# Three half-size products in place of four in the lower left quarter of a Toeplitz convolution, with the low half of the operand made by an adding transfer

## What is computed

```python
kv = jnp.einsum('bhil,bhjl->bijhl', k_, v_)          # here k = v = ctx: symmetric in i, j
y = irfft(rfft(kv, n=2 * L) * rfft(ssm_kernel, n=2 * L))[..., :L]   # causal convolution along l
out = y + kv * D[None, None, None, :, None]
out = jnp.einsum('bijhl,bhil->bjhl', out, q_)         # q = layernorm(x)
x = x + jnp.tanh(g_xattn[0]) * out
```

## Time and profile before

| | |
|---|---|
| median of 3 runs | 4437.81 us (4437.43 to 4440.19) |
| the profiled execution's own time | 4438.08 us |
| span of its trace | 4436.3 us |
| mean granted TensorE clock | 0.991 |
| TensorE busy | 4317.6 us, 97% of the span |
| VectorE busy | 2749.1 us, 62% (nearly all the time up to 2120 us, about a quarter behind) |
| ScalarE busy | 1477.2 us, 33% |
| GpSimd busy | 879.4 us, 20% |
| the 16 transfer engines | some 38% of the span |

### The profile page before, as it was taken

The page is one execution under the profiler, slowest core; times in us unless marked ns, Lnnn a source line. Parts: engine busy times, 40 slices in busy tenths (PEclk is TensorE's granted clock), DMA queues, the critical chain, the costliest instruction groups (busy, mean ns, idle before and its releaser), DMA issues.

```text
span 4436.3 us, 72403 instructions
## 1 busy us (share of the span) xinstructions
PE 4317.6 (97%) x27466; PEld 3963.1 (89%) x27466; DVE 2749.1 (62%) x2977; ACT 1477.2 (33%) x2003; POOL 879.4 (20%) x1072
## 2 busy tenths in 40 slices
PE   7999999999999999999599999999999999999997
PEld 7999999999999999999478887888898988988986
DVE  7999999999999999999443442222233233233232
ACT  4555554555545555454211111111121121121120
POOL 1222222222122222222000004443001111111111
PEclk9999999999999999999799999999999999999999
DMA  3333333333334333333713233344244344344332
GB/s 108 114 118 106 115 111 113 118 109 114 109 113 118 109 115 109 112 118 90 138 58 114 77 95 100 98 106 111 74 140 99 76 114 99 76 114 99 76 95 48
DMA packets 227122, 457.67 MB, mean 103 GB/s; under 512 B 41744, under 2 KB 107770, under 8 KB 226998
## 3 DMA queue, kind: packets, MB, share of 16 engines
q1 hardware_dynamic: 200150, 388.45, 30.4%
q0 software_dynamic: 26848, 67.41, 7.5%
HBM read 285.86 MB, written 169.89 MB: 103 GB/s over the span
## 4 chain that ended last, share of the span: by engine, by line
PE 47%; DMA 2%; DVE 1%; issue 1%; ACT 0%; SPq 0%; POOL 0%; DVEq 0%; POOLq 0%; ACTq 0%
PE moe_ps L1497 11%; PE moe_ps L1498 11%; PE moe_ps L1499 11%; PE moe_ps L1515 4%; PE moe_ps L1517 4%; PE moe_ps L1516 4%; PE moe_psT L1486 1%; DMA out<-moe_y,moe_add_i 1%; DMA out<-moe_y 1%; DVE moe_zl L1395 1%; DMA moe_y<-out 0%; ACT moe_zh L1167 0%; DVE moe_hid L1408 0%; DVE moe_y L1422 0%; DMA moe_zin<-zT_d 0%
## 5 line engine op out<-in xcount | busy, mean ns | idle before, releaser
L592 PE MATMUL att_psY<-att_kv_hi,att_tz_hi 128*128 128x288 f32 x4608 | 1395.5, 303 | 31.5 <-DVE att_kv_lo L463 31.5
L593 PE MATMUL att_psY<-att_kv_lo,att_tz_hi 128*128 128x288 f32 x4608 | 1359.7, 295 | 0.0
L594 PE MATMUL att_psY<-att_kv_hi,att_tz_lo 128*128 128x288 f32 x4608 | 1355.9, 294 | 0.0
L592 PEld LDWEIGHTS att_psY<-att_kv_hi,att_tz_hi 128*128 128x128 f32 x4608 | 865.3, 188 | 43.7 <-issue 43.7
L1497 PE MATMUL moe_ps<-moe_zh,moe_w1h 128*128 128x512 f32 (+2 forms) x2368 | 860.6, 363 | 33.6 <-DVE moe_zl L1395 21.8
L594 PEld LDWEIGHTS att_psY<-att_kv_hi,att_tz_lo 128*128 128x128 f32 x4608 | 868.0, 188 | 0.0
L593 PEld LDWEIGHTS att_psY<-att_kv_lo,att_tz_hi 128*128 128x128 f32 x4608 | 867.6, 188 | 0.0
L1498 PE MATMUL moe_ps<-moe_zl,moe_w1h 128*128 128x512 f32 (+2 forms) x2368 | 858.8, 363 | 0.0
L1499 PE MATMUL moe_ps<-moe_zh,moe_w1l 128*128 128x512 f32 (+2 forms) x2368 | 856.4, 362 | 0.0
L1408 DVE TENSOR_TENSOR moe_hid<-moe_ps,moe_act_s 128x512 f32<-128x512 f32 (+2 forms) x148 | 91.6, 619 | 882.3 <-PE moe_ps L1499 857.9
L352 ACT ACTIVATE att_y<-att_psY 128x576 f32<-128x576 f32 x512 | 332.1, 649 | 703.7 <-PE att_psY L594 702.9
(11 more groups left out here) (168 smaller groups left out, 5213.8 us busy)
## 6 DMA issues: line engine op xcount, KB each, us to landing
att_kT<-in_cT SPq DMA_DIRECT2D x64, 512.0 KB, 4.2
att_xn<-in_x SPq DMA_DIRECT2D x64, 512.0 KB, 5.8
att_tz_hi<-filt_hi SPq DMA_DIRECT2D x64, 512.0 KB, 3.7
att_tz_lo<-filt_lo SPq DMA_DIRECT2D x64, 512.0 KB, 4.8
out<-att_x SPq DMA_DIRECT2D x64, 512.0 KB, 4.0
z_d<-att_z SPq DMA_DIRECT2D x64, 512.0 KB, 3.7
zT_d<-att_zT SPq DMA_DIRECT2D x64, 512.0 KB, 4.9
moe_zin<-zT_d SPq DMA_DIRECT2D x64, 512.0 KB
```

Source lines behind the costliest of these rows:

```text
L592: nc.tensor.matmul(acc, tz_hi[u][:, d:d + P], hi, start=(c == 0), stop=False)
L593: nc.tensor.matmul(acc, tz_hi[u][:, d:d + P], lo, start=False, stop=False)
L594: last = nc.tensor.matmul(acc, tz_lo[u][:, d:d + P], hi, start=False, stop=(c == a))
```

## The change

The lower left quarter of the matrix (sums a = 4 to 7, key tiles c = 0 to 3) has 16 block products, built from T1 to T7. The change computes it with three products of half the size. With d(0) = k(0) - k(2) and d(1) = k(1) - k(3) it forms V0 = T4 d(0) + T3 d(1) and V1 = T5 d(0) + T4 d(1) (function `shared`). Sum 4 is V0 plus S-blocks on k(2), k(3) plus its own T-blocks, sum 6 is minus V0 plus S-blocks on k(0), k(1) plus its own; sums 5 and 7 do the same with V1. The S-blocks are S(d) = T(d) + T(d-2), made once for all heads in `prepare_filters`. That is 12 block products for the quarter, and 32 for the head.

What comes with it: `differences` and `low_u` on VectorE (L568, L576; 1152 elements a partition), `high_u` on ScalarE (L418), and `minus_v` on ScalarE (L435, four copies of 288 columns a head), which writes the negative of V from `psY[0]` to `psY[1]` in PSUM. The far sums are built on top of it, in the order 0, 1, 2, 3, 4, 6, 5, 7. The Toeplitz arrays shrink to 768 columns each, and `load_sums` fetches two arrays of 640 columns into one buffer.

The low part of half 1 of `kv` is no longer subtracted by VectorE. ScalarE writes -kv_hi into `kv_lo` (`minus_high`, L410), and GpSimd issues a transfer of 1152 KB that adds `kv` to it in SBUF (`add_low`, L355). The fifth sum, `pairs(.., 1)` and `squares(.., 1)` wait for its landing (`lo_in`).

The hand-written orders change as well. VectorE begins a step with `pairs(h+1, 0)` and the statistics of x; `low(h+1)` and `low_u(h+1)` stand at its end. ScalarE begins with the squares, and rounds half 0 between the first two sums. On TensorE `turn_o(h-1, 0)` and `turn_z(h-2, 1)` move behind the second sum of the next head, and `turn_o(h-1, 1)` between the two halves of the sixth.

```diff
...
+TAPS = 896
+SUMS = 768
+PAD = TAPS + SUMS
...
+    TW = 6 * P
+    SW = 5 * P
+    def toeplitz(filt, first, width):
+        return bass.AP(filt.tensor, first, [[PAD, H], [1, P], [1, width]])
+    t_hi, t_lo = toeplitz(filt_hi, 0, TW), toeplitz(filt_lo, 0, TW)
+    s_hi, s_lo = toeplitz(filt_hi, TAPS, SW), toeplitz(filt_lo, TAPS, SW)
+    ORDER = (0, 1, 2, 3, 4, 6, 5, 7)
+    def blocks(a):
+        if a < G:
+            return [("T", a - c, c) for c in range(a + 1)]
+        far = [("S", a + 2 - c, c) for c in (2, 3)] if a < 6 else [("S", a - c, c) for c in (0, 1)]
+        return far + [("T", a - c, c) for c in range(G, a + 1)]
...
+            def load_sums(h):
+                wait(sp, y_done, NT * h)
+                sp.dma_start(sz_hi[:, :].bitcast(F32), s_hi[h]).then_inc(sz_in, 16)
+                sp.dma_start(sz_lo[:, :].bitcast(F32), s_lo[h]).then_inc(sz_in, 16)
...
+            def add_low(h, u):
+                pool.wait_ge(minus_set, h + 1)
+                pool.sem_inc(passed, 1)
+                nc.gpsimd.dma_start(
+                    kv_lo[u][:, keys_of(1)].rearrange("p t b i -> p (t b i)").rearrange("p (x n) -> p x n", x=2).bitcast(F32),
+                    kv[1][:, :, :, :].rearrange("p t b i -> p (t b i)").rearrange("p (x n) -> p x n", x=2),
+                    accum_op=ALU.add, max_dma_last_dim=8192).then_inc(lo_in, 16)
+            add_low(0, 0)
             def step(h, u, ahead, back, back2):
+                roots(0, h)
                 if back:
                     roots(1, h - 1)
                 if ahead:
-                    roots(0, h + 1)
+                    add_low(h + 1, 1 - u)
...
+            def minus_high(h, u):
+                act.wait_ge(hi_set, 2 * h + 2)
+                nc.scalar.activation(kv_lo[u][:, keys_of(1)].rearrange("p t b i -> p (t b i)"),
+                                     kv_hi[u][:, keys_of(1)].rearrange("p t b i -> p (t b i)").bitcast(F32),
+                                     ACT.Copy, scale=-1.0).then_inc(minus_set, 1)
...
+            def conv_out(h, n):
+                a = ORDER[n]
+                act.wait_ge(y_done, NT * h + n + 1)
+                if n % G == 0:
+                    wait(act, multiplied, 2 * (h - 1) + n // G + 1)
                 nc.scalar.activation(y[a // G][:, a % G].rearrange("p (c b) i -> p c (b i)", c=2),
-                                     psY[a % 2][:, :, 0:NB * PAIRS], ACT.Copy).then_inc(y_set, 1)
+                                     psY[n % 2][:, :, 0:NB * PAIRS], ACT.Copy).then_inc(y_set, 1)
+            def minus_v(h, k, half):
+                act.wait_ge(v_done, 4 * h + 2 * k + half + 1)
+                if half == 0:
+                    act.wait_ge(y_set, NT * h + G + 2 * k)
+                nc.scalar.activation(psY[1][:, half, 0:NB * PAIRS], psY[0][:, half, 0:NB * PAIRS], ACT.Copy,
+                                     scale=-1.0).then_inc(v_set, 1)
...
+                more = not (isinstance(h, int) and h >= H - 2)
+                if ahead:
+                    squares(h + 1, 0)
+                conv_out(h, 0)
+                if ahead:
+                    high(h + 1, 1 - u, 0)
+                conv_out(h, 1)
                 if back2:
                     columns(h - 2, 1)
-                conv_out(h, 0)
-                if ahead:
-                    keys(h + 1)
-                conv_out(h, 1)
-                if ahead:
-                    keys_on(h + 1)
+                conv_out(h, 2)
+                normal_x(h, u)
+                conv_out(h, 3)
+                minus_v(h, 0, 0)
+                minus_v(h, 0, 1)
+                queries(h, u, 0)
                 if back2:
                     gate_parts(h - 2)
-                normal_x(h, u)
-                if ahead:
-                    squares(h + 1, 0)
-                conv_out(h, 2)
-                queries(h, u, 0)
-                if ahead:
-                    high(h + 1, 1 - u, 0)
-                conv_out(h, 3)
-                queries(h, u, 1)
                 if ahead:
                     squares(h + 1, 1)
                 conv_out(h, 4)
+                queries(h, u, 1)
                 if ahead:
                     high(h + 1, 1 - u, 1)
                 conv_out(h, 5)
+                minus_v(h, 1, 0)
+                minus_v(h, 1, 1)
                 if back:
                     normal_x1(h - 1)
+                if ahead:
+                    minus_high(h + 1, 1 - u)
                 conv_out(h, 6)
+                if ahead:
+                    high_u(h + 1)
                 if back:
                     columns(h - 1, 0)
+                if more:
+                    keys(h + 2)
                 conv_out(h, 7)
+                if more:
+                    keys_on(h + 2)
...
+            def differences(h):
+                dve.wait_ge(kv_set, 2 * h + 1)
+                dve.wait_ge(sq_set, 2 * h + 1)
+                nc.vector.tensor_tensor(diff[:, :, :, :].rearrange("p t b i -> p (t b i)"),
+                                        kv[0][:, 2:4].rearrange("p t b i -> p (t b i)"),
+                                        kv[0][:, 0:2].rearrange("p t b i -> p (t b i)"),
+                                        ALU.subtract).then_inc(u_set, 1)
...
+                if ahead:
+                    pairs(h + 1, 0)
+                tell_x(h, u)
                 if back:
                     residual(h - 1, 1 - u, 0)
                     multiply(h - 1, 1 - u, 1)
-                if ahead:
-                    pairs(h + 1, 0)
-                if back:
                     add_up(h - 1, 1)
                 if ahead:
                     pairs(h + 1, 1)
-                    low(h + 1, 1 - u, 0)
                 if back2:
                     logits(h - 2)
                 if back:
                     residual(h - 1, 1 - u, 1)
                 multiply(h, u, 0)
+                if ahead:
+                    differences(h + 1)
                 add_up(h, 0)
                 if ahead:
-                    tell_x(h + 1, 1 - u)
-                    low(h + 1, 1 - u, 1)
+                    low(h + 1, 1 - u)
+                    low_u(h + 1)
...
+            def thrice(acc, w_hi, w_lo, d, x_hi, x_lo, start, stop):
+                cols = slice(d * P, (d + 1) * P)
+                nc.tensor.matmul(acc, w_hi[:, cols], x_hi, start=start, stop=False, skip_group_check=True)
+                nc.tensor.matmul(acc, w_hi[:, cols], x_lo, start=False, stop=False, skip_group_check=True)
+                return nc.tensor.matmul(acc, w_lo[:, cols], x_hi, start=False, stop=stop, skip_group_check=True)
+            def half_of(t, tile, half):
+                return t[:, tile, half * NB:(half + 1) * NB, :].rearrange("p b i -> p (b i)")
+            def conv(h, u, n, between=None):
+                a = ORDER[n]
+                if n == 0:
+                    pe.wait_ge(lo_set, h + 1)
+                if n == G:
+                    pe.wait_ge(lo_in, 16 * h + 16)
+                    pe.wait_ge(sz_in, 32 * h + 32)
+                if a < G:
+                    wait(pe, y_set, NT * h + n - 1)
+                terms = blocks(a)
+                for half in range(2):
+                    acc = psY[n % 2][:, half, 0:NB * PAIRS]
+                    if a >= G:
+                        pe.wait_ge(v_set, 4 * h + (2 if a % 2 else 0) + half + 1)
+                    for k, (kind, d, c) in enumerate(terms):
+                        w_hi, w_lo, first = (tz_hi[u], tz_lo[u], 0) if kind == "T" else (sz_hi, sz_lo, 3)
+                        last = thrice(acc, w_hi, w_lo, d - first, half_of(kv_hi[u], NT - 1 - c, half),
+                                      half_of(kv_lo[u], NT - 1 - c, half), k == 0 and a < G, k == len(terms) - 1)
+                    if half == 0 and between is not None:
+                        between()
...
+            def shared(h, u, k):
+                if k == 0:
+                    pe.wait_ge(u_hi_set, h + 1)
+                    pe.wait_ge(u_lo_set, h + 1)
+                pe.wait_ge(y_set, NT * h + 3 + 2 * k)
+                for half in range(2):
+                    acc = psY[0][:, half, 0:NB * PAIRS]
+                    for c in range(2):
+                        last = thrice(acc, tz_hi[u], tz_lo[u], G + k - c, half_of(u_hi, 1 - c, half),
+                                      half_of(u_lo, 1 - c, half), c == 0, c == 1)
+                    last.then_inc(v_done, 1)
 
             def turn_x(h, half):
...
             def step(h, u, ahead, back, back2):
                 conv(h, u, 0)
                 conv(h, u, 1)
+                if back:
+                    turn_o(h - 1, 0)
+                if back2:
+                    turn_z(h - 2, 1)
+                conv(h, u, 2)
+                conv(h, u, 3)
                 if back2:
                     gates(h - 2)
-                conv(h, u, 2)
+                shared(h, u, 0)
+                turn_x(h, 0)
+                conv(h, u, 4)
                 if back2:
                     sum_gates(h - 2)
```

(11 more changed lines are left out.)

103 lines of the change are left out of this document (60 added, 43 removed).

## The result

The changed kernel takes 4475.7 us (median, 4474.0 to 4477.1), the one before 4439.0 us (4437.4 to 4441.9): a ratio of 1.0082, 95% interval 1.0064 to 1.0099. It is slower by 0.8%, where 4428 us and a small gain were forecast. That lies inside the wide range of 4394 to 4500 and outside the 4418 to 4442 that the forecast's own path was given.

A forecast was written before the change was run, and what follows sets the result against it. TensorE was taken to bound the kernel at 32.50 us a head, VectorE close behind at 31.9. From 4438 us, 8 came off for the ring over 62 heads and 2 for the last head's tail: 4428 us, range 4394 to 4500.

The forecast's parts named there:

- the forecast's own path: Whole kernel: the ring binds and the adding transfer is hidden; 4428 us, range 4418 to 4442, chance 0.48.
- the cover of the wait for z: Second half of TensorE's head: 1.6 us of slack before the next start cover `turn_z`'s wait, priced at nothing.
- The ring: Closed chain through VectorE, ScalarE and TensorE from one `low` to the next: it binds, 32.37 us a head, 0.13 less.
- wait for `turn_o`: VectorE before the second `residual`: it gets there about 0.5 us too early and is released by `turn_o`.
- The edge through ScalarE: TensorE before sum 3: it waits about 0.3 us for ScalarE's copy, queued behind `high`, and goes on at 8.57.
- VectorE's own work: VectorE's instructions in a head without waits: 31.9 us, as full as before the change.
- the adding transfer is hidden: Transfer of 1152 KB at 11.5 us (7 to 16): with the loads it lands after about 15 of 16.8 us.
- Rival (b): Adding transfer lands late, so the fifth sum waits: 4552 us with 2 us late, at worst 4800; chance 0.20.
- Rival (c): GpSimd can't issue the adding transfer beside VectorE's two-operand work: late by 2.8 us, 4602 us; chance 0.10.
- Rival (a): The ring is looser, so VectorE alone sets the head at 31.9 us: 4399 us; chance 0.22.

The follow-up runs named there:

- e5: Changed kernel with 16 products that nobody reads on TensorE ahead of the wait for z in `turn_z(h-1, 0)`: 4445.7 us, ratio 1.0010.
- e10: e5 with the keys' copy `keys_on(h+2)` ahead of the last sum's copy in ScalarE's order: 4429.3 us, ratio 0.9978.
- e3: Changed kernel with `turn_o(h-1, 1)` ahead of the sixth sum instead of between its halves: 4431.5 us, ratio 0.9982.
- e12: Changed kernel with the adding transfer undone: VectorE subtracts low half 1 again behind `low_u`, without `minus_high`: 4618.8 us, ratio 1.0409.
- e11: Changed kernel with the edits of e3, e5 and e10 together: 4418.2 us, ratio 0.9953.
- e4: Changed kernel with the adding transfer cut to 128 of 1152 columns of each row: 4475.2 us, ratio 1.0074.
- e6: Changed kernel with `turn_z(h-1, 0)` behind the last sum and 20 transposes of the identity ahead of the head's first wait: 4474.0 us, ratio 1.0070.
- e9: e6 with the adding transfer cut to 128 of its 1152 columns per row: 4426.2 us, ratio 0.9967.
- e8: Changed kernel with VectorE waiting before `multiply(h, 0)` for the first step of GpSimd's root of the head before: 4533.9 us, ratio 1.0205.

## Why the prediction was wrong

**The step that failed** is the cover of the wait for z, "its 1.6 us of slack cover the wait of `turn_z` for z". It priced TensorE's freed time at nothing wherever no engine waited for it. TensorE does get there with time to spare, and the idle time itself is what costs. Around the end of the pause the granted clock goes to 0.50 and 1.4 us are lost, which the slack that was left doesn't cover. Two smaller errors helped. z was forecast at 26.8 (as 6.55 after `residual`) and comes at 28.45 in every odd head, 8.2 after `residual`. The head that the 6.55 was read from had only the second step of the root beside the multiply, while its first took 0.19 us. Here the first step starts 0.06 us too late and takes 2.28. A start so close to the multiply's was never priced. And I looked at TensorE's next start only, not at the copies behind the last sum: `keys_on` stands behind one, and `pairs` waits for it.

**The price, term by term.** Before 32.50 us a head. The ring alone gives 32.34 (-0.16, forecast -0.13). The late z adds 0.37 to the even heads, 0.18 in the mean (e5: 32.52), most of it through the keys' copy (e10: 32.36). The low clock adds the rest, 33.08 - 32.52 = 0.56 in the mean, 35 us of the total. Without the clock's fall the change would have been a draw, as e5 is.

**Right: the ring.** 32.37 forecast, 32.34 measured, `residual` at 20.24 against 20.27, and a wait for `turn_o` of 0.31 us where 0.5 stood. The edge through ScalarE is there too: its copy, queued behind `high`, ends 8.53 us after the `low` at 985.68, and sum 3 begins at 8.58, where 8.57 was forecast. TensorE's own wait there is about half of the 0.3 us that was forecast.

```profile
993.58 0.63 ACT L427 ACTIVATE att_y<-att_psY 128x576 f32<-128x576 f32 x1
993.98 0.29 PE L695 MATMUL att_psY<-att_kv_hi,att_tz_lo 128*128 128x288 f32 x1
994.26 0.40 PE L693 MATMUL att_psY<-att_kv_hi,att_tz_hi 128*128 128x288 f32 x1
```

e3 takes 0.38 out of it and e12 puts 2.5 in; the head follows both times. VectorE's own work, 31.9 forecast, is what the odd heads of e3 and e11 show (31.96, 31.95).

**Right: the adding transfer is hidden.** 10.4 us from issue to landing, against 11.5 taken and bounds of 7 and 16. The 10.4 are near the middle that was taken for want of a row, which is luck. e4 shows that its price doesn't matter here. e6 and e9 show that the margin of 4.0 us or more is gone once the loads are issued ahead of the transfer. Rival (b) is false for this kernel and true for a neighbour of it. Rival (c) is dead: the issue starts 0.6 us after `minus_high` and takes 1.24 us beside VectorE's two-operand work (1017.99 in GpSimd's timeline), so it isn't held up until that work ends. The Trainium skill ("SBUF — State Buffer", who interferes with whom) says that such work holds up a GpSimd instruction that reads SBUF, and not one that only writes it; this trace agrees with both, 2.28 us for the one-column step and 1.24 for the issue. The Trainium skill's fit ("DMA: Bandwidth & Descriptors", anatomy of a DMA on the GpSimd path), which gave an estimated 4.7 us, is less than half of the 10.4 measured.

**Rival (a)** was false: the ring binds, until `turn_o` is moved.

**What stays open.** Why 7 of the 29 pauses of 3.0 us don't have the low clock behind them. All 29 are of the same length to 0.01 us, so it isn't their length that decides. And what exactly brings it on: a pause of 1.8 us at the head's start is harmless in the changed kernel (0 of 29), and one of 2.2 us, 7 us behind another of 1.5, isn't in e8 (55 of 58). No single length of one pause explains both, and I didn't try pauses of set lengths by themselves, nor did I look for the 0.38 us by which e11's even heads are longer than its odd ones.

## What to carry to other kernels

Work taken from a full TensorE comes back as idle time, and idle time is not free: ask where it will collect, how long the pause is there, and what is queued behind the matmuls that follow it. Where a forecast rests on "x us of slack", price the case that the work behind it runs at the 1.2 GHz level. If a pause can't be avoided, matmuls that nobody reads can hold the clock (e5: 30 us for 16 of them per head); better is to spend the freed time by pulling forward what the bound engine waits for (e3), and to take copies that others wait for out from behind the last sum (e10).

## What the hardware did that I hadn't expected

- A pause of 3.0 us, with 24 us of matmuls and no wait above 0.2 us ahead of it (988.36 to 1012.5), is enough for 3.1 us at the 1.2 GHz level (0.24 us a matmul in place of 0.13). The fall can come 1.4 us after the work has begun again, and the granted clock of the pause itself then reads 1.00. After other pauses of the same length it comes 0.3 us before their end, or not at all.
- Less than 0.1 us decides whether a one-column step of GpSimd takes 0.19 or 2.28 us (0.01 before the multiply or 0.06 behind it). From head 4 to 61 the odd heads lost this race every time and the even ones won it.
- What an adding transfer inside SBUF took went by which was issued first, it or the loads. One of 1152 KB takes 10.4 us where the loads come behind it and 14.5 to 16.3 where they come first, and one of 128 KB takes 3.2 and 8.5 to 10.6 us in the same two orders. The loads pay too: the keys' 512 KB take 9.2 us, and 6.9 with most of the transfer left out (e4). Before they took 4.2. In the changed kernel nothing waited for them.
